# Three graph convolutions: node work done visit by visit inside the neighbour sums

## The chip, the cores and the metric

The kernel runs on one core of a Trainium2 chip. The metric is device microseconds (us) of one execution; shown are the median and the extremes of three executions. One further execution was profiled, and all rows below come from it.

## The reference, cut to what matters

The input is a graph of 12500 nodes with 32 features each and 200000 edges, sorted by destination. Four blocks follow one another, each of the form `x = x + block(relu(layernorm(x)))`: three graph convolutions in a row, an attention over edges, a relational convolution, and a tensor product. The change touches only the first block and the entry of the second:

```python
def _gcn_conv(x, src, dst, norm, W, b, n_nodes):
    h = x @ W
    msg = h[src] * norm[:, None]          # norm = dinv[src] * dinv[dst], self loops included
    out = jax.ops.segment_sum(msg, dst, num_segments=n_nodes)
    return out + b
h = jax.nn.relu(_gcn_conv(h, src, dst, norm, W1, b1, n))   # 32 -> 128
h = jax.nn.relu(_gcn_conv(h, src, dst, norm, W2, b2, n))   # 128 -> 128
h = jax.nn.relu(_gcn_conv(h, src, dst, norm, W3, b3, n))   # 128 -> 32
...
x = x + gcn;  h = relu(layernorm(x));  x = x + attention(h)   # its q, k, v are h @ Wq, h @ Wk, h @ Wv
```

All is float32. The kernel sums before or after the product with W, whichever is narrower, so its three neighbour sums are 32, 128 and 32 features wide.

## The kernel before, in words

Nodes lie in 98 tiles of 128 (J; arrays are padded to JP = 104). Edges lie in 98 groups (NG) of 2048: 128 partitions by 16 columns (GT). Since edges are sorted by destination, a group meets one to three node tiles; each meeting is a pair, called a visit here. There are 195 pairs and one empty visit, NS = 196. The table `group_words`, made once by `group_tables`, holds for each visit its group (W_NEED), its tile (W_TILE) and its ring slot (W_SLOT), and for each group the last visit that reads it (W_DONE).

A neighbour sum is `group_sums` (L907). Its engines run side by side, each in its own program order, held together by semaphores:

- GpSimd (POOL) issues 16 indirect DMAs for each group (L884), each of which gathers one row per partition from a DRAM table into a ring of two slots. A row is the float32 value split in three bfloat16 parts. POOL waits for `released`, which SyncE raises (L902) when ScalarE has copied the last visit of the group that held the slot. SyncE also stages the indices (L871) and counts landed groups (L897).
- ScalarE copies the slot into `rows`, one of two buffers, once for each visit (L945, and L944 for two columns of marks in the first sum).
- VectorE compares column numbers with the destinations and so makes a one-hot matrix in bfloat16 for each visit (L865), two visits ahead, in one of two buffers. After the products it joins the three parts (L959) and adds the result into the visit's tile of `sums` (L966).
- TensorE multiplies 16 one-hots with 16 columns of rows and accumulates them in PSUM (L979).

A sum ends with a barrier of all engines. Between sums the node work is done on all tiles at once: the own value of each node is added, `node_linear` (L1080) turns each tile with TensorE, multiplies it by the weights and copies it back, `on_vector` (L1191) applies scale, bias and relu in a chain of VectorE instructions, `store_parts` (L1048) splits the result in three parts and stores the table that the next sum gathers from. After the third sum come the residual, the layer norm of attention (`norm_relu`, L1006), the q, k, v product and the store of the key and value table `tab64`. `step_tables` (L490), which makes the per-edge tables that only later passes read, runs before `group_tables`.

The order is written out by hand; no planner is involved. The score pass of attention (L1302) begins with its own gathers on POOL.

Of the kernel before, what the change touches and what calls it, by code (L numbers as in the profile page):

```python
# [19 lines left out]
F32 = mybir.dt.float32  # L20
BF16 = mybir.dt.bfloat16
# [687 lines left out]
def group_tables(nc, k, dram):  # L709
# [3 lines left out]
    with ExitStack() as ctx:  # L713
# [28 lines left out]
        with nc.Block() as block:  # L742
# [17 lines left out]
            def _(dve):  # L760
# [24 lines left out]
                chain.link(nc.vector.memset(words[:, W_DONE, :], 1.0))  # L785
                chain.link(nc.vector.tensor_single_scalar(words[:, W_DONE, 0:NG], done[:], 1.0, op=ALU.add))
# [4 lines left out]
                nc.vector.tensor_single_scalar(shift[:], spread[:, 1, :], -float(P), op=ALU.mult).then_inc(set_up, 1)  # L791
                for c in range(NG // CH):
# [68 lines left out]


def _group_one_hot(nc, k, out, step):

    return nc.vector.tensor_tensor(out[:], k["columns"][:],  # L865
                                   k["group_rel"][:, bass.ds(step * GT, GT)].unsqueeze(1).to_broadcast([P, P, GT]), ALU.is_equal)


def _stage_half(sp, k, staged, indexed, turn, half):

    sp.dma_start(staged[:, half * HALF * GT:(half + 1) * HALF * GT],  # L871
                 k["group_src"][:, bass.ds((turn * SPAN + half * HALF) * GT, HALF * GT)]).then_inc(indexed[half], DMA)


def _gather_groups(nc, pool, table, staged, ring, slots, indexed, released, gathered, entered):

    with pool.Fori(0, ROUNDS) as i:
        for q in range(SPAN):
            if q % HALF == 0:
                pool.wait_ge(indexed[q // HALF], (i + 1) * DMA)  # L880
            pool.wait_ge(released, i * SPAN + q + 1)
            pool.sem_inc(entered, 1)
            for g in range(GT):
                nc.gpsimd.indirect_dma_start(  # L884
                    out=ring[:, q % slots, g, :], out_offset=None, in_=table,
                    in_offset=bass.IndirectOffsetOnAxis(ap=staged[:, q * GT + g:q * GT + g + 1], axis=0)).then_inc(gathered[q % HALF], DMA)


def _pass_groups(sp, k, staged, slots, indexed, gathered, landed, copied, released):

    sp.sem_inc(released, slots)
    for half in range(2):
        _stage_half(sp, k, staged, indexed, 0, half)
    with sp.Fori(0, ROUNDS) as i:
        for q in range(SPAN):
            sp.wait_ge(gathered[q % HALF], (i * 2 + q // HALF + 1) * GT * DMA)
            sp.sem_inc(landed, 1)  # L897
            if q % HALF == HALF - 1:
                _stage_half(sp, k, staged, indexed, i + 1, q // HALF)
            done = sp.value_load(k["group_words"][0:1, W_DONE, bass.ds(i * SPAN + q, 1)], min_val=1, max_val=NS)  # L900
            sp.wait_ge(copied, done)
            sp.sem_inc(released, 1)  # L902
    for half in range(2):
        sp.wait_ge(indexed[half], (ROUNDS + 1) * DMA)


def group_sums(nc, k, name, table, sums, width, marks=None, last=None):  # L907

    W = 3 * width
    held = W + (2 if marks is not None else 0)  # L910
    slots = 2
    with ExitStack() as ctx:
        sb, psum, sem = _scope(nc, ctx, name)
        staged = sb("staged", [P, SPAN * GT], U32)
        ring = sb("ring", [P, slots, GT, W], BF16)
        rows = [sb(f"rows{h}", [P, GT, held], BF16) for h in range(2)]
        onehot = [sb(f"onehot{h}", [P, P, GT], BF16) for h in range(2)]
        joined = [sb(f"joined{h}", [P, width]) for h in range(2)]
# [1290 lines left out]
```

## Time and profile before

| | us |
|---|---|
| Median of three executions | 16398.22 |
| Lowest and highest | 16385.13 and 16399.88 |
| Profiled execution, its time | 16390.01 |
| Its span | 16388.3 |
| POOL busy | 10536.2 (64%) |
| TensorE matmuls busy | 7263.1 (44%) |
| VectorE busy | 5726.5 (35%) |
| ScalarE busy | 2889.0 (18%) |
| Mean granted TensorE clock | 0.645 of full speed |

The engines' busy shares are means over stages that have different limits. To read them by stage, one asks for the busy time of each engine in stretches of the span, and for the order of instructions at the seams between stretches. In such a row the columns are the stretch, its length, then the busy time and instruction count of TensorE matmuls, TensorE weight loads, VectorE, ScalarE and POOL, the granted clock as a share of full speed, the busy share of the DMA engines and GB/s. In a timeline row the columns are start, duration, engine, line, operation, operands, count, and in brackets the idle time before it and what ended it.

### The profile page before, as it was taken

Reading aid. Unit: us, or ns where it says so; the run is one execution under the profiler, and the core shown is the slowest. Engines: PE = TensorE matmul, PEld = TensorE weight load, DVE = VectorE, ACT = ScalarE, POOL = GpSimd, SP = SyncE. Lnnn points to the kernel's source line nnn. Section 1 sums busy time; section 2 is a strip of 40 time slices with the busy share of each in tenths; the row PEclk is TensorE's granted clock in tenths of the full one; section 3 lists DMA queues with packets and bytes.
Section 4 is the critical chain, followed back from the end, with each engine's and each line's share of the span. In section 5 each row is a group of like instructions: output and inputs, shape, how many; then the busy total and the mean of one; then the engine's idle time right before and its main releaser. Section 6 shows DMA issues by size and latency. Waiting matters only on the chain. (4 is left out here: it accounts for less than half of the span.)

```text
span 16388.3 us, 210648 instructions
## 1 busy us (share of the span) xinstructions
PE 7263.1 (44%) x43306; PEld 5194.0 (32%) x43356; DVE 5726.5 (35%) x10642; ACT 2889.0 (18%) x3659; POOL 10536.2 (64%) x10566
## 2 busy tenths in 40 slices
PE   2311111233333111115555535558889867455556
PEld 1111111122222111114444423335555536333435
DVE  4511113111113111121111147767777742323332
ACT  1111111455551111110000000012222211000001
POOL 0377774677772777767777743346666652777774
PEclk8655555677675555555555555579999975777676
DMA  4111111322221111112222212211111112111112
GB/s 145 19 19 19 19 19 36 85 77 77 77 77 26 19 19 19 19 15 52 49 49 49 49 32 67 67 31 33 33 33 33 33 40 58 21 21 21 21 21 48
DMA packets 652644, 675.65 MB, mean 41 GB/s; under 512 B 303477, under 2 KB 489790, under 8 KB 649663
## 3 DMA queue, kind: packets, MB, share of 16 engines
q0 software_dynamic: 340624, 383.65, 12.6%
q1 hardware_dynamic: 280958, 278.52, 5.6%
q10 hardware_dynamic: 30384, 7.79, 0.3%
q14 instruction: 661, 5.41, 0.1%
q8 instruction: 17, 0.28, 0.0%
HBM read 517.39 MB, written 149.11 MB: 41 GB/s over the span
## 5 line engine op out<-in xcount | busy, mean ns | idle before, releaser
L884 POOL DMA_INDIRECT gcn_sum_ring<-scratch_parts,gcn_sum_staged x4704 | 4684.5, 996 | 1961.9 <-issue 1395.6
L979 PE MATMUL gcn_sum_totals<-gcn_sum_rows,gcn_sum_onehot 128*128 128x98 bf16 (+2 forms) x9408 | 1290.0, 319 | 5113.9 <-ACT gcn_sum_rows L945 5107.2
L979 PEld LDWEIGHTS gcn_sum_totals<-gcn_sum_rows,gcn_sum_onehot 128*128 128x128 bf16 x9408 | 973.0, 158 | 5431.5 <-issue 5365.5
L865 DVE TENSOR_TENSOR gcn_sum_onehot<-k_columns,k_group_rel 128x2048 bf16<-128x2048 bf16 x594 | 728.5, 1227 | 5041.1 <-PE gcn_sum_totals L979 4863.1
L703 POOL DMA_INDIRECT sh_ring<-scratch_tab,sh_staged x1664 | 1879.4, 1129 | 830.1 <-issue 506.9
L703 POOL DMA_INDIRECT rel_ring<-scratch_tab,rel_staged x1664 | 1702.4, 1023 | 832.5 <-issue 476.1
L945 ACT COPY gcn_sum_rows<-gcn_sum_ring 128x1536 bf16 (+1 forms) x588 | 1604.6, 2751 | 2924.3 <-SPq L897 2916.4
L1339 POOL DMA_INDIRECT score_ring<-scratch_tab,score_staged x1664 | 1737.5, 1044 | 533.2 <-issue 506.8
L642 PE MATMUL sh_accumulator<-sh_message,sh_onehot 128*128 128x248 f32 x3328 | 1209.7, 543 | 1245.6 <-DVE sh_message L2002 1242.4
L642 PE MATMUL rel_accumulator<-rel_message,rel_onehot 128*128 128x512 f32 x3328 | 1609.3, 628 | 2.8 <-ACT rel_accumulator L675 2.8
L642 PEld LDWEIGHTS sh_accumulator<-sh_message,sh_onehot 128*128 128x128 f32 x3328 | 950.6, 293 | 1504.1 <-issue 1326.4
L1748 DVE TENSOR_TENSOR rel_message<-rel_coef,rel_ring 128x512 f32<-128x512 f32 x1664 | 1044.9, 690 | 14.2
L1379 PE MATMUL score_q_edge<-att_h,score_onehot_t 128*128 x3328 | 752.4, 402 | 272.9 <-ACT score_onehot_t L1328 272.9
L642 PEld LDWEIGHTS rel_accumulator<-rel_message,rel_onehot 128*128 128x128 f32 x3328 | 635.1, 201 | 660.0 <-issue 654.6
L1379 PEld LDWEIGHTS score_q_edge<-att_h,score_onehot_t 128*128 128x128 f32 x3328 | 725.4, 330 | 355.2 <-issue 355.2
L1999 DVE TENSOR_TENSOR sh_message<-sh_parts,sh_ring 128x1024 f32<-128x1024 f32 x208 | 257.3, 1237 | 1659.5 <-DMA sh_ring<-scratch_tab,sh_staged 1659.5
L1373 PE MATMUL score_flipped_ps<-k_ident,score_onehot 128*128 128x128 f32 x1664 | 409.2, 427 | 822.5 <-DVE score_onehot L591 822.5
L1357 DVE TENSOR_TENSOR score_product<-score_q_edge,score_ring 128x256 f32<-128x256 f32 x208 | 88.4, 425 | 1779.4 <-DMA score_ring<-scratch_tab,score_staged 1779.4
L1598 POOL TENSOR_TENSOR value_message<-value_ring,att_score 128x256 f32<-128x256 f32 x208 | 183.3, 881 | 683.3 <-DVE value_parts L1622 478.8
L642 PE MATMUL value_accumulator<-value_parts,value_onehot 128*128 128x36 bf16 x4992 | 448.1, 199 | 371.3 <-issue 201.2
L1373 PEld LDWEIGHTS score_flipped_ps<-k_ident,score_onehot 128*128 128x128 f32 x1664 | 326.7, 224 | 850.3 <-DVE score_onehot L591 616.8
L1328 ACT COPY score_onehot_t<-score_flipped_ps 128x1024 f32<-128x1024 f32 x208 | 210.6, 1012 | 2043.6 <-PE score_flipped_ps L1373 2043.6
(393 smaller groups left out, 9375.7 us busy)
## 6 DMA issues: line engine op xcount, KB each, us to landing
gcn_sum_ring<-scratch_parts,gcn_sum_staged POOLq DMA_INDIRECT x4704
scratch_kv<-score_ring SPq DMA_DIRECT2D x208, 256.0 KB, 2.0
value_ring<-scratch_kv SPq DMA_DIRECT2D x208, 256.0 KB, 2.6
rel_ring<-scratch_tab,rel_staged POOLq DMA_INDIRECT x1672
score_ring<-scratch_tab,score_staged POOLq DMA_INDIRECT x1664, 2.5
sh_ring<-scratch_tab,sh_staged POOLq DMA_INDIRECT x1664, 2.4
scratch_totals<-rel_taken SPq DMA_DIRECT2D x102, 256.0 KB
rlo_lin_chunk<-scratch_totals SPq DMA_DIRECT2D x98, 256.0 KB, 2.9
```

The source lines that it names most:

```text
L642: last = self.nc.tensor.matmul(into, onehot, part, start=False, stop=True, skip_group_check=True)
L703: nc.gpsimd.indirect_dma_start(out=ring[:, q, g, :], out_offset=None, in_=table, in_offset=bass.IndirectOffsetOnAxis(ap=staged[:, q, g:g + ...
L865: return nc.vector.tensor_tensor(out[:], k["columns"][:], k["group_rel"][:, bass.ds(step * GT, GT)].unsqueeze(1).to_broadcast([P, P, GT]), ...
L884: nc.gpsimd.indirect_dma_start(out=ring[:, q % slots, g, :], out_offset=None, in_=table, in_offset=bass.IndirectOffsetOnAxis(ap=staged[:, ...
L945: nc.scalar.copy(rows[q % 2][:, :, 0:W], ring[:, bass.ds(slot, 1), :, :].rearrange("p o g w -> p (o g) w")).then_inc(copied, 1)
L979: done = nc.tensor.matmul(totals[:, q, 0:held], onehot[q % 2][:, :, g], rows[q % 2][:, g, :], start=(g == 0), stop=(g == GT - 1))
L1328: nc.scalar.copy(onehot_t[q % 2][:], flipped_ps[:, q % 2, :, :]).then_inc(turned[q], 1)
L1339: nc.gpsimd.indirect_dma_start(out=ring[:, q, g, :], out_offset=None, in_=dram["tab64"], in_offset=bass.IndirectOffsetOnAxis(ap=staged[:, ...
L1373: last = nc.tensor.transpose(flipped_ps[:, q % 2, g, :], onehot[q % 2][:, g, :], k["ident"][:])
L1379: last = nc.tensor.matmul(q_edge[:, q % 2, g * D:(g + 1) * D], onehot_t[q % 2][:, g, :], q_nodes[:, bass.ds(tiles[g] * D, D)], start=True, ...
L1748: nc.vector.tensor_tensor(message[m % 2][:, g, :].rearrange("p (b f) -> p b f", f=D), coef[m % 2][:, g, :].unsqueeze(2).to_broadcast([P, N ...
L1999: nc.vector.tensor_tensor(m[:, :, 0:4 * D].rearrange("p g (c f) -> p g c f", f=D), parts[:, q, :, 0:4].unsqueeze(3).to_broadcast([P, G, 4, ...
```

## The change

- The three sums become three functions, `first_sums`, `second_sums` and `third_sums`, that share a class `Gathered`. It holds what `group_sums` held: gathers, SyncE's control, the copies, the one-hots and the products are issued as before, with two PSUM buffers in place of four.
- The joined result is no longer added into an array of all tiles. A running sum of one tile is kept, `sums = sums * keep + joined`, where `keep` is 1 if this visit has the tile of the visit before, else 0.
- Behind it, each visit does the node work of its tile with the sum as it stands, a few visits late (`lag`): own value, dinv, a TensorE transpose, the weights, relu, the split in parts, and a store of 128 rows to the table, issued on ScalarE's queue. Where a tile has two visits, the later one overwrites what the earlier one stored. The third sum does residual, layer norm, q, k, v and the store of keys and values in this way.
- Removed: the node work between the sums, the clearing of the arrays of sums, the store and reload of the wide own values (`tab128`), and the node work at the entry of attention.
- Weights are loaded once, ahead of the first sum. The bias b1 is a 33rd row of W1, b2 is a product of a row of ones with b2.
- `step_tables` is moved behind the third sum. `group_tables` makes `keep`. W_DONE counts from an offset (BASE = 16).

The core of the diff:

```diff
-        group_sums(nc, k, "gcn_sum0", dram["parts32"], sums, D, marks=k["marks"], last=last)
...
-        node_linear(nc, k, "gcn_lin1", sums[:].rearrange("p j f -> p (j f)"), JP // 4, 1, w1, wide[:].rearrange("p j f -> p (j f)"))
-        on_vector(nc, "gcn_act1", [
...
-        store_parts(nc, "gcn_parts1", dram["parts128"], wide, HID)
-        store_table(nc, "gcn_table1", dram["tab128"], wide, HID)
...
+    def fold(self, dve, k, m, q):
+
+        dve.wait_ge(self.multiplied, m + 1 + BASE)
+        self.nc.vector.tensor_reduce(self.joined[q % 2][:], self.totals[:, q % 2, 0:3 * self.width].rearrange("p (c f) -> p f c", c=3),
+                                     axis=AX_X, op=ALU.add).then_inc(self.folding, 1)
+        dve.wait_ge(self.folding, m + 1)
+        self.nc.vector.scalar_tensor_tensor(out=self.sums[q % 2][:], in0=self.sums[(q + 1) % 2][:], scalar=k["keep"][:, bass.ds(m, 1)],
+                                            in1=self.joined[q % 2][:], op0=ALU.mult, op1=ALU.add).then_inc(self.folded, 1)
...
+            _linked(dve, scaling, m + 1, nc.vector.tensor_tensor(held[q % 2][:], got.sums[q % 2][:], _tile(h, tile), ALU.add))
+            dve.wait_ge(flipped, m - 1 + BASE)
+            nc.vector.tensor_scalar(scaled[q % 2][:], held[q % 2][:], k["dinv"][:, bass.ds(tile, 1)], None, ALU.mult).then_inc(summed, 1)
+
+        def split_rows(dve, m, q):
...
+            nc.vector.tensor_copy(_tile(wide, tile), raised[q % 2][:])
+            _linked(dve, splitting, 2 * m + 1, nc.vector.tensor_tensor(rest[q % 2][:], raised[q % 2][:], high, ALU.subtract))
+            _linked(dve, splitting, 2 * m + 2, nc.vector.tensor_copy(middle, rest[q % 2][:]))
+            nc.vector.tensor_tensor(low, rest[q % 2][:], middle, ALU.subtract).then_inc(split, 1)
...
+            nc.scalar.activation(parts[q][:, 0:HID], linear_ps[:, 0:HID], ACT.Relu, scale=k["dinv"][:, bass.ds(tile, 1)]).then_inc(activated, 1)
...
+            act.dma_start(dram["parts128"][bass.ds(tile * P, P), :], parts[q][:]).then_inc(stored, DMA)
...
@@ second_sums, ScalarE @@
+                def body(n, q):
+                    if _live(n, 0):
+                        got.copy_rows(act, k, n, q)
+                    if _live(n, 2):
+                        turn(act, n - 2, (q + 2) % 4)
+                    if _live(n, 3):
+                        activate(act, n - 3, (q + 1) % 4)
+                    if _live(n, 4):
+                        turn_again(act, n - 4, q)
+                    if _live(n, 7):
+                        store(act, n - 7, (q + 1) % 4)
...
@@ third_sums, VectorE @@
+                def body(n, q):
+                    if _live(n, 0):
+                        got.make_one_hot(dve, k, n, q)
+                    if _live(n, 2):
+                        normalize(dve, n - 2, (q + 2) % 4)
+                    if _live(n, 1):
+                        add_own(dve, n - 1, (q + 3) % 4)
+                    if _live(n, 4):
+                        take_query(dve, n - 4, q)
```

In the third sum `add_own` is the fold and nine more VectorE instructions, each waiting for the one before (own value, scale with bias, relu with residual, mean, centring, square, variance), and `normalize` three (reciprocal, scale with relu, add to x).

## Rows read from the trace of the kernel before

**Rows 1.** Stretches: us, PE, PEld, DVE, ACT, POOL busy, clock, DMA, GB/s.
```profile
192.50:282.50 90.00, 36.11 (x156) 31.12 (x156) 17.76 (x83) 28.71 (x39) 12.33 (x13) 0.65 0.79 258
561.00:634.90 73.90, 0.00 (x0) 0.00 (x0) 47.13 (x43) 0.29 (x1) 0.03 (x1) 0.50 0.34 56
634.90:2709.10 2074.20, 290.04 (x3088) 257.27 (x3088) 343.89 (x965) 303.76 (x386) 1596.43 (x1568) 0.51 0.14 19
2709.10:2910.40 201.30, 35.56 (x126) 17.23 (x126) 126.86 (x80) 10.44 (x32) 7.51 (x27) 0.59 0.27 82
2910.40:4914.90 2004.50, 699.08 (x3088) 448.52 (x3088) 384.00 (x579) 1016.15 (x193) 1527.04 (x1568) 0.70 0.29 77
4914.90:5244.50 329.60, 149.42 (x636) 106.22 (x636) 129.85 (x247) 61.09 (x199) 55.94 (x196) 0.61 0.11 28
5244.50:7283.20 2038.70, 280.42 (x3088) 252.18 (x3088) 306.05 (x579) 280.51 (x193) 1560.94 (x1568) 0.51 0.14 19
7283.20:7406.20 123.00, 30.52 (x126) 17.64 (x126) 63.90 (x56) 10.42 (x30) 7.44 (x26) 0.62 0.12 28
```

**Rows 2.** Costliest groups, gathers and a one-hot: busy us, mean ns, idle.
```profile
L884 POOL DMA_INDIRECT gcn_sum_ring<-scratch_parts,gcn_sum_staged x4704 | 4684.5, 996 | 1961.9 <-issue 1395.6
L1339 POOL DMA_INDIRECT score_ring<-scratch_tab,score_staged x1664 | 1737.5, 1044 | 533.2 <-issue 506.8
...
L591 DVE TENSOR_TENSOR score_onehot<-k_iota,k_drel 128x1024 f32<-128x1024 f32 x209 | 254.4, 1218 | 5.2
```

**Rows 3.** Second sum, POOL's waits: us, times, longest; line 884: ns least/median/greatest.
```profile
POOL gcn_sum_ring L884 <- issue: 453.9, 1490, 0.3
POOL gcn_sum_ring L884 <- SPq L902: 23.4, 77, 0.3
...
L884 POOL DMA_INDIRECT gcn_sum_ring<-scratch_parts,gcn_sum_staged x4704: 940/944/1991, 634.9 to 7282.1; - x196
```

**Rows 4.** Timeline, first sum: two gathers beside one-hots.
```profile
659.69 1.23 DVE L865 TENSOR_TENSOR gcn_sum_onehot<-k_columns,k_group_rel 128x2048 bf16<-128x2048 bf16 x1 [25.30 <-PE gcn_sum_totals L979]
659.86 1.87 POOL L884 DMA_INDIRECT gcn_sum_ring<-scratch_parts,gcn_sum_staged  x1 [0.30 <-issue]
...
662.73 1.23 DVE L865 TENSOR_TENSOR gcn_sum_onehot<-k_columns,k_group_rel 128x2048 bf16<-128x2048 bf16 x1 [1.12 <-issue]
663.28 1.49 POOL L884 DMA_INDIRECT gcn_sum_ring<-scratch_parts,gcn_sum_staged  x1 [0.30 <-issue]
```

**Rows 5.** Timeline, second sum: ScalarE's copies of one group.
```profile
3400.16 0.94 POOL L884 DMA_INDIRECT gcn_sum_ring<-scratch_parts,gcn_sum_staged  x1 [0.30 <-issue]
3401.82 10.53 ACT L945 COPY gcn_sum_rows<-gcn_sum_ring 128x6144 bf16 x2 [9.61 <-SPq L897]
```

**Rows 6.** Timeline, end of the first sum.
```profile
2707.97 0.94 POOL L884 DMA_INDIRECT gcn_sum_ring<-scratch_parts,gcn_sum_staged  x1 [0.30 <-issue]
2710.89 1.47 ACT L945 COPY gcn_sum_rows<-gcn_sum_ring 128x1536 bf16 x1
2716.81 1.22 DVE L865 TENSOR_TENSOR gcn_sum_onehot<-k_columns,k_group_rel 128x2048 bf16<-128x2048 bf16 x1 [0.73 <-issue]
2722.38 0.48 DVE L1164 MEMSET gcn_w<- 128x512 f32 x1 [0.99 <-PEq L99]
```

**Rows 7.** Timeline, end of the second sum: ScalarE.
```profile
4916.90 15.75 ACT L945 COPY gcn_sum_rows<-gcn_sum_ring 128x6144 bf16 x3 [15.23 <-SPq L897]
```

**Rows 8.** Timeline, start of the second sum.
```profile
2906.57 1.16 SPq L871 DMA_DIRECT2D gcn_sum_staged<-k_group_src  x2
2910.31 0.97 POOL L884 DMA_INDIRECT gcn_sum_ring<-scratch_parts,gcn_sum_staged  x1 [142.84 <-DMA gcn_sum_staged<-k_group_src]
```

**Rows 9.** Groups by shape, 561 to 7404 us: small operations.
```profile
L966 DVE TENSOR_TENSOR gcn_sums<-gcn_sums,gcn_sum_joined 128x32 f32 x392 | 75.3, 192 | 28.0
L966 DVE TENSOR_TENSOR gcn_sums<-gcn_sums,gcn_sum_joined 128x128 f32 x196 | 57.3, 292 | 28.0
L1126 PE MATMUL gcn_lin_flipped_ps<-k_ident,gcn_lin_chunk 128*128 128x128 f32 x222 | 62.1, 374 | 132.1 <-POOL gcn_lin_chunk L1116 129.4
L1143 ACT COPY gcn_lin_turned<-gcn_lin_flipped_ps 128x128 f32<-128x128 f32 x222 | 51.1, 267 | 281.8 <-PE gcn_lin_flipped_ps L1126 281.8
```

More of the change, by code:

```diff
@@ L860, in _ @@
                 nc.scalar.activation(k["dinv"][:], k["dinv"][:], ACT.Sqrt)
[L863 to L872, printed above, removed]
@@ L875, in _gather_groups @@
[L875 to L886, printed above, removed]
@@ L889, in _pass_groups @@
[L889 to L904, printed above, removed]
@@ L1238, in gcn, with _live, _pairs, _word_of @@
-def gcn(nc, io, k, dram):
+BASE, AHEAD = 16, 8
+def _live(n, lag):
+    return not isinstance(n, int) or 0 <= n - lag < NS
+def _pairs(engine, body, lag):
+    for n in range(AHEAD):
+        body(n, n % 4)
+    with engine.Fori(0, (NS - AHEAD) // 4) as i:
+        for q in range(4):
+            body(i * 4 + q + AHEAD, q)
+    for n in range(NS, NS + lag):
+        body(n, n % 4)
+def _word_of(engine, k, row, n, low, high):
+    return engine.value_load(k["group_words"][0:1, row, bass.ds(n, 1)], min_val=low, max_val=high)
@@ new lines, in _tile_of, with _tile, _pair_one_hot, _gather_groups @@
+def _tile_of(engine, k, n):
+    return _word_of(engine, k, W_TILE, n, 0, J)
+def _tile(a, tile):
+    return a[:, bass.ds(tile, 1), :].rearrange("p o f -> p (o f)")
+def _pair_one_hot(nc, k, out, n):
+    return nc.vector.tensor_tensor(out[:], k["columns"][:],
+                                   k["group_rel"][:, bass.ds(n * GT, GT)].unsqueeze(1).to_broadcast([P, P, GT]), ALU.is_equal)
+def _gather_groups(nc, pool, table, staged, ring, slots, indexed, released, gathered, entered):
+    with pool.Fori(0, ROUNDS) as i:
+        for q in range(SPAN):
+            if q % HALF == 0:
+                pool.wait_ge(indexed[q // HALF], (i + 1) * DMA)
+            pool.wait_ge(released, i * SPAN + q + 1)
+            pool.sem_inc(entered, 1)
+            for g in range(GT):
+                nc.gpsimd.indirect_dma_start(
+                    out=ring[:, q % slots, g, :], out_offset=None, in_=table,
+                    in_offset=bass.IndirectOffsetOnAxis(ap=staged[:, q * GT + g:q * GT + g + 1], axis=0)).then_inc(gathered[q % HALF], DMA)
@@ new lines, in _stage_half, with _pass_groups @@
+def _stage_half(sp, k, staged, indexed, turn, half):
+    sp.dma_start(staged[:, half * HALF * GT:(half + 1) * HALF * GT],
+                 k["group_src"][:, bass.ds((turn * SPAN + half * HALF) * GT, HALF * GT)]).then_inc(indexed[half], DMA)
+def _pass_groups(sp, k, staged, slots, indexed, gathered, landed, copied, released):
+    sp.sem_inc(released, slots)
+    for half in range(2):
+        _stage_half(sp, k, staged, indexed, 0, half)
+    with sp.Fori(0, ROUNDS) as i:
+        for q in range(SPAN):
+            sp.wait_ge(gathered[q % HALF], (i * 2 + q // HALF + 1) * GT * DMA)
+            sp.sem_inc(landed, 1)
+            if q % HALF == HALF - 1:
+                _stage_half(sp, k, staged, indexed, i + 1, q // HALF)
+            done = sp.value_load(k["group_words"][0:1, W_DONE, bass.ds(i * SPAN + q, 1)], min_val=BASE + 1, max_val=NS + BASE)
+            sp.wait_ge(copied, done)
+            sp.sem_inc(released, 1)
+    for half in range(2):
+        sp.wait_ge(indexed[half], (ROUNDS + 1) * DMA)
@@ L1283, in gcn @@
[L1283 to L1293 removed]
+        w1 = sb("w1", [D + 1, HID])
```

599 lines of the change are left out of this document (428 added, 171 removed).

## The prediction, made before the result was known

> **What bounds the kernel now.** I first asked for the busy times by stretch, because the busy shares of the whole span mix stages. The three neighbour sums take 2074, 2004 and 2039 us, and in each POOL is busy 1527 to 1596 us while no other engine passes 1016 [rows 1]. POOL's idle time there is about 477 us in each sum, 0.30 us ahead of each of 1568 gathers, and no single idle time is longer [rows 1, 3]: it never waits for a slot. So a sum is bound by issuing gathers, one each 0.944 + 0.305 = 1.249 us [rows 3, 4], 1958 us in all, plus what lengthens single gathers. A gather has a median of 944 ns and a greatest of 1991 [rows 3]; the lengthening is 1596 - 1568 x 0.944 = 116 us in the first sum, 47 in the second, 81 in the third [rows 1], together 244.
>
> Then I read the seams. Between the last gather of one sum and the first of the next there are 201.3, 329.6 and (to attention's first gather) 123.0 us, in which POOL does 7.5, 56 and 7.4 us of copies [rows 1]. Node work lies open there. These 654 us are what the change can take; the sums' 6117 us are what it can spoil.
>
> **Removed and added at the seams.** What stays of a seam is the drain of the last visits and the setup of the next sum.
>
> - First seam. The last gather ends at 2708.9, the copies start 1.8 us later, and the old sum was over at 2721.4 (the next instruction, at 2722.38, had idled 0.99) [rows 6]. Now three visits and their late steps drain. ScalarE needs for a visit a copy of 1.47, a turn of 0.27, two activations of some 0.3 and a store's issue of 0.4 to 0.6 (SyncE's two took 1.16 [rows 8]), with register loads 3.9 us; VectorE needs a one-hot of 1.23, five small operations of the fold and four of the split at 0.16 to 0.29 [rows 4, 9], with loads about 4.5 us. The last copy ends 9.5 us after the first starts, its products 1.5 later, its fold at 13, then flip 0.4, turn 0.3, product 0.4, activations 0.7, split 1.7, store about 2.5: 19.5 us. The three small steps on `last`, with barriers of about 1 us, take 3, and from staging to first gather 3.7 us pass [rows 8]. Sum 1.8 + 19.5 + 3 + 3.7 = 28. Gain 173.
> - Second seam. Three copies took 15.75 us [rows 7]; with 2.3 us of new ScalarE work between them they take 20.5. Products of 3.6, fold 2, flip, turn, two products, activation, second flip and turn, narrow product (each 0.27 to 0.4 [rows 9], with signals 4.5), split and store 3.7: 34. With landing, barrier and staging 39.5. Gain 290.
> - Third seam. Bound by VectorE: one-hot 1.23, some fourteen small operations at about 0.22 with the wait between them, and three register loads of up to 0.7 (0.73 is the idle ahead of a one-hot [rows 6]) make about 7 us for a visit. The drain is 24 us, with landing and barriers 28. Gain 95. Residual, norm, q, k, v and table store lie within this seam's 123 us and go.
> - `step_tables` moves past the sums. It takes 90.0 us with nothing beside it [rows 1] and will take the same between the third sum and attention: its 13 gathers on POOL, its transposes and its SyncE stores have no neighbour in either place. 0; if SyncE's stores were late, at most a few us.
> - Front. Nine weight loads at 0.4 us issue each plus about 3 us to land, less a cleared array of 2.8 us: +5.
>
> Seams and front: 173 + 290 + 95 - 5 = 553 us gained.
>
> **Added beside the gathers.** All per-visit work lies beside POOL's 1.249 us beat. A group takes about 20.4 us and mostly has two visits, so an engine has 10.2 us for one.
>
> - ScalarE, second sum: 5.3 for the copy [rows 5] and about 2.3 of new work, 7.6 us. Its order decides when the ring slot is released. The next group's first gather began at 3400.16, the group's two copies ended at 3412.35 [rows 5], and POOL needs their slot 16 gathers, 20.0 us, after 3400.16: 7.8 us are spare and 2.3 are used. In a group of three visits the copies alone take 15.75 and 4.6 come between: late by about 2 us, in the few such groups. +4. The stores queue on ScalarE, each waits for the one before, and a copy queued behind would wait; a visit lies between them, so I take 0, at worst 2 us a visit, within the 7.8.
> - VectorE: 4.5, 5 and 7 us a visit. TensorE adds two to four float32 operations of 0.37 us [rows 9] to 16 products of about 0.22. Both under 10.2. What is queued behind the new waits are the next visits' products and one-hots; POOL does not wait for those while copies go through.
> - Lengthened gathers. This is the price that counts. At 659.86 a gather that starts 0.17 us after a one-hot takes 1.87 us, and at 663.28 one takes 1.49; both end 0.81 us after the one-hot's end (660.92 and 663.96) [rows 4]. So a gather needs something at about 0.13 us after its start that the one-hot holds until it ends. If phases are spread evenly, an operation of d us covers that instant with chance d/1.25 and costs d/2, thus d²/2.5: 0.605 us for a one-hot, 119 a sum. Measured: 116, 47, 81, or 244/588 = 0.415 us for each. In the score loop, whose one-hots are as long, the lengthening is (1044 - 944) ns x 1664 = 166 us, 0.80 for each of 208 [rows 2]. The order of VectorE's work is new, so I do not keep 0.415 but go toward the even value and take 588 x 0.5 = 294; bounds 0.24 (the second sum now, 141) and 0.80 (the score loop, 470). The small operations with SBUF operands, about seven a visit at 0.19 to 0.29 [rows 9], cost by the same formula 0.014 to 0.034 each, 82 us; I take 60, since some fall where a gather has just been held up. Bounds 0 and, if each held the gather for its whole length, 4.35 us over the three sums' visits x 196 = 853. Term: 294 + 60 - 244 = +110.
>
> The row on the one-hot is weighed against the Trainium skill, page "SBUF — State Buffer", section "Who interferes with whom": a tensor_tensor with two SBUF inputs blocks only GpSimd instructions that read SBUF, and descriptor generation is inferred not to suffer; copies, casts and tensor_scalar in a two-port mode do block it, for their whole length. The trace disagrees on the one-hot, a tensor_tensor: it lengthens gathers. By the page the new subtractions and additions would be free and the term 30 us lower, and only the new copies, casts and scalings would count.
>
> **Sum.** 16390.0 - 553 + 4 + 110 = 15951, with the 8 us by which the median stands above the profiled execution 15959. I forecast 15960. By the bounds of the lengthening that are likely: 15,850 (one-hots at 0.24, small ones at half) to 16,110 (0.80).
>
> **Rivals.**
> - A. Small operations hold the gathers fully, so that every new VectorE instruction is paid on POOL: + 853 - 60 on the forecast, 16,750, slower. It decides from (553 - 4 + 244 - 294)/588 = 0.85 us more a visit. For it: the one-hot does block until its end [rows 4], and the page on SBUF quoted above says so of two-port operations. Against: a gather begun first ran on unhindered, and the median stays at 944 [rows 3]. 5%.
> - B. An in-order engine can't do a visit in 10.2 us, and POOL waits for slots: likeliest ScalarE in the second sum, waiting behind stores, or VectorE in the third. At 11.5 us a visit in one sum the price is 1.3 x 196 = 255: 16,215. Against: the 7.6 and 7 above. 6%.
> - C. The drains are deep: each of five to seven late steps waits for the slowest engine, 60 us more a seam: 16,140. For it: 8 to 14 waits along one visit. 8%.
> - D. The new order falls into a phase that spares the gathers, as the second sum now: 588 x 0.24 + 20 - 244 = -83 in place of +110: 15,770. 8%.
>
> The forecast has 73%. The 80% range 15,850 to 16,110 reaches halfway to C and D. Less than 0.2% (33 us) can't be told from no change here. Faster by more: all but A and some of B, 93%; same 2%; slower 5%.
>
> **What would show it.** Steps: first gathers of the second and third sum 28 and 40 us after the last of the sum before; step_tables 90 us, now after the third sum; POOL's idle in each sum still near 477 us, and none by SyncE's release; POOL's busy sum in the three loops near 4440 + 354 = 4800 us. I am wrong if POOL's idle grows (B), if its busy sum passes 5100 (A), or if a seam is over 80 us (C).

## The result, and the profile after

The changed kernel takes 15,866.2 us (median of four, 15,846.7 to 15,883.2); the kernel before took 16,399.1 beside it. The ratio is 0.9675, 95% interval 0.9664 to 0.9687. The profiled execution, 15,883.2 us, is the slowest of the four; its span is 15,881.5, 506.8 less than before. In five of the runs below (e1 to e4 and h1) the kernel before, too, took some 19,300 us, so that their times can't be set beside the others.

The stretches, as in [rows 1]; the last row is `step_tables`, now inside the third seam:

```profile
471.00:548.80 77.80, 0.00 (x0) 0.00 (x0) 45.16 (x47) 0.29 (x1) 0.07 (x1) 0.50 0.33 55
548.80:2574.50 2025.70, 473.65 (x3662) 364.62 (x3662) 593.32 (x1918) 433.63 (x957) 1548.03 (x1568) 0.50 0.16 29
2574.50:2604.30 29.80, 9.28 (x62) 6.79 (x62) 12.98 (x46) 9.15 (x23) 0.13 (x1) 0.50 0.11 33
2604.30:4671.00 2066.70, 1234.07 (x4612) 721.17 (x4612) 696.26 (x1905) 1145.98 (x763) 1577.34 (x1568) 0.70 0.29 77
4671.00:4724.10 53.10, 25.88 (x92) 16.06 (x92) 14.92 (x56) 20.49 (x21) 0.10 (x1) 0.60 0.04 10
4724.10:6770.50 2046.40, 466.53 (x3659) 358.99 (x3659) 818.33 (x3066) 372.51 (x763) 1568.74 (x1568) 0.50 0.14 22
6770.50:6899.70 129.20, 45.91 (x221) 37.81 (x221) 34.62 (x154) 36.33 (x60) 12.31 (x14) 0.51 0.57 182
6808.20:6898.20 90.00, 35.72 (x156) 30.52 (x156) 17.70 (x82) 28.64 (x39) 12.19 (x13) 0.52 0.80 258
```

The seams went from 201.3, 329.6 and 123.0 us to 29.8, 53.1 and 39.2 (129.2 less the 90.0 of `step_tables`), the front from 73.9 to 77.8: 531.8 - 3.9 = 527.9 us gained. The three sums grew from 6117.4 to 6138.8 us, +21. Net 506.5, the difference of the spans.

What the +21 is, the profile's rows for the gathers tell (busy us, mean ns of one, idle us before them):

```profile
L1136 POOL DMA_INDIRECT sum0g_ring<-scratch_parts,sum0g_staged x1568 | 1548.1, 987 | 833.9 <-issue 832.1
L1136 POOL DMA_INDIRECT sum1g_ring<-scratch_parts,sum1g_staged x1568 | 1577.5, 1006 | 519.1 <-issue 472.2
L1136 POOL DMA_INDIRECT sum2g_ring<-scratch_parts,sum2g_staged x1568 | 1568.8, 1001 | 530.7 <-issue 461.4
```

Busy less 1568 x 0.944 is the lengthening: 68, 97 and 89 us, together 254, where before had 116, 47 and 81, together 244 [rows 1, 3]. The other part is a wait that before did not have. The second sum's waits (us, times, longest):

```profile
PE sum_narrow_ps L1470 <- DVE sum_parts L1419: 520.9, 188, 3.1
ACT sum_turned_again L1438 <- PE sum_narrow_ps L1470: 233.1, 91, 3.1
POOL sum1g_ring L1136 <- SPq L1160: 17.1, 18, 5.1
```

The last row is POOL waiting for a ring slot: 17.1 less 18 usual pauses of 0.305 leaves 11.6 us. The other two rows name its cause, and the end of that sum shows it in single instructions:

```profile
4678.82 5.33 ACT L1197 COPY sum1g_rows<-sum1g_ring 128x6144 bf16 x1
...
4686.72 0.19 DVE L1419 TENSOR_TENSOR sum_parts<-sum_rest,sum_parts 128x32 bf16<-128x32 f32 x1
...
4687.05 0.60 PE L1470 MATMUL sum_narrow_ps<-gcn_w,sum_turned_again 128*128 128x32 f32 x2 [2.86 <-DVE sum_parts L1419]
...
4687.69 0.27 ACT L1438 COPY sum_turned_again<-sum_flipped_again_ps 128x128 f32<-128x128 f32 x1 [3.06 <-PE sum_narrow_ps L1470]
...
4690.30 5.31 ACT L1197 COPY sum1g_rows<-sum1g_ring 128x6144 bf16 x1 [2.34 <-DMA scratch_parts<-sum_parts]
```

TensorE's narrow product of visit n-4 waits until VectorE has split visit n-5, and VectorE does that only a turn later, behind its fold. ScalarE's second turn waits for the narrow product, and its next copy stands in line behind: 11.5 us from one copy's start to the next, where the copy takes 5.3.

### The profile page after: what moved, and what is told of

It is laid out like the page before. It is cut to its first block and busy times, and to the rows that moved or that the text cites. A ratio compares the mean times of both kernels' runs of the same rounds, so it can differ in the third digit from the quotient of the medians.

```text
span 15881.5 us, 235812 instructions
## 1 busy us (share of the span) xinstructions
PE 8010.6 (50%) x45355; PEld 5572.4 (35%) x45356; DVE 6520.0 (41%) x15205; ACT 3194.9 (20%) x5174; POOL 10462.7 (66%) x10318
## 5 line engine op out<-in xcount | busy, mean ns | idle before, releaser
L703 POOL DMA_INDIRECT sh_ring<-scratch_tab,sh_staged x1664 | 1875.2, 1127 | 830.2 <-issue 506.8
L1136 POOL DMA_INDIRECT sum0g_ring<-scratch_parts,sum0g_staged x1568 | 1548.1, 987 | 833.9 <-issue 832.1
L1136 POOL DMA_INDIRECT sum1g_ring<-scratch_parts,sum1g_staged x1568 | 1577.5, 1006 | 519.1 <-issue 472.2
L1136 POOL DMA_INDIRECT sum2g_ring<-scratch_parts,sum2g_staged x1568 | 1568.8, 1001 | 530.7 <-issue 461.4
L1197 ACT COPY sum1g_rows<-sum1g_ring 128x6144 bf16 x196 | 1042.1, 5318 | 680.0 <-SPq L1155 599.7
L1211 PE MATMUL sum0g_totals<-sum0g_rows,sum0g_onehot 128*128 128x98 bf16 x3136 | 299.5, 285 | 1638.7 <-ACT sum0g_rows L1197 1638.7
L1211 PE MATMUL sum1g_totals<-sum1g_rows,sum1g_onehot 128*128 128x384 bf16 x3136 | 944.5, 487 | 331.6 <-ACT sum1g_rows L1197 325.8
L1809 PE MATMUL score_q_edge<-k_q,score_onehot_t 128*128 x3328 | 752.6, 402 | 272.7 <-ACT score_onehot_t L1758 272.7
L1809 PEld LDWEIGHTS score_q_edge<-k_q,score_onehot_t 128*128 128x128 f32 x3328 | 725.5, 331 | 355.2 <-issue 355.2
L1211 PE MATMUL sum2g_totals<-sum2g_rows,sum2g_onehot 128*128 128x96 bf16 x3136 | 294.4, 283 | 886.2 <-ACT sum2g_rows L1197 818.2
L1211 PEld LDWEIGHTS sum1g_totals<-sum1g_rows,sum1g_onehot 128*128 128x128 bf16 x3136 | 492.2, 163 | 709.6 <-issue 413.3
```

The costliest lines, as they stand in the source:

```text
L703: nc.gpsimd.indirect_dma_start(out=ring[:, q, g, :], out_offset=None, in_=table, in_offset=bass.IndirectOffsetOnAxis(ap=staged[:, q, g:g + ...
L1136: nc.gpsimd.indirect_dma_start(out=ring[:, q % slots, g, :], out_offset=None, in_=table, in_offset=bass.IndirectOffsetOnAxis(ap=staged[:, ...
L1197: self.nc.scalar.copy(self.rows[q % 2][:, :, 0:3 * self.width], self.ring[:, bass.ds(slot, 1), :, :].rearrange("p o g w -> p (o g) w")).th ...
L1211: last = self.nc.tensor.matmul(self.totals[:, q % 2, 0:self.held], self.onehot[q % 2][:, :, g], self.rows[q % 2][:, g, :], start=(g == 0), ...
L1809: last = nc.tensor.matmul(q_edge[:, q % 2, g * D:(g + 1) * D], onehot_t[q % 2][:, g, :], q_nodes[:, bass.ds(tiles[g] * D, D)], start=True, ...
```

## The experiments

In the profiles of e1 to e4 and of h1 register instructions on VectorE, ScalarE, TensorE and SyncE lasted several times as long in bursts (in h1 the mean of VectorE's assert instruction was 0.122 us against 0.023), and POOL waited for slots. These profiles are read for how single gathers stand to single VectorE operations. Their sums of lengthening can be compared with each other only: e3 had 145 us and f3, the same kernel, 269, perhaps because POOL's waits change where the gathers fall; no run shows that.

**The gathers' lengthening: no one-hot, quarters, and a third lever (e1 to e4).**

```diff
# e1: later visits of sums 2 and 3 reuse what the buffer holds
-        _pair_one_hot(...).then_inc(self.made, 1)
+        dve.sem_inc(self.made, 1)
# e2: quarters
+        for c in range(0, P, 32):
+            last = nc.vector.tensor_tensor(onehot[:, c:c + 32, :], k["columns"][:, c:c + 32, :], ..., ALU.is_equal)
# e3: second sum, VectorE
-                    if _live(n, 6):
-                        split_rows(dve, n - 6, (q + 2) % 4)
+                    if _live(n, 5):
+                        split_rows(dve, n - 5, (q + 3) % 4)
# e4: quarters, and in sums 1 and 3 the column numbers lie in PSUM
+        self.columns = psum("columns", [P, 4, P // 4, GT]) if width == D else None
```

> The changed kernel without the one-hots of the second and third sum, save the first two of each: stale one-hots are multiplied, so those sums are wrong numbers. Theory T1: the lengthening of gathers beside the new per-visit work comes from the 1.23 us one-hots alone; the lengthening beyond 0.944 us a gather falls from 97 and 89 us in those two sums to under 15 us each, and is about 68 us as before in the first, which keeps its one-hots; total 15866 - 160 = 15705. Theory T2: the new small operations (0.16 to 0.35 us each, 9 to 15 a visit) carry a share by the d*d/2.5 formula of the prediction; then 25 to 30 us stay in each of the two sums, total about 15740. Theory T3: small operations hold gathers for their whole length: over 200 us would stay in each; already unlikely.

> The changed kernel with each one-hot made in four instructions of 32 nodes (about 0.35 us each) instead of one of 1.23 us, in all three sums. T1, each instruction holds back only a gather whose early instant falls into it, until that instruction ends: a hit costs at most 0.35 us instead of 1.23, so the lengthening falls from 254 us to 588 x 4 x 0.35*0.35/2.5 = 115 us or less: total about 15730 to 15780. Rival: instructions back to back hold the gather as one (it gets in only when VectorE pauses): lengthening unchanged or larger, 15870 to 15930.

> Second sum only: split_rows runs five visits late instead of six. In the changed kernel TensorE's narrow product of visit n-4 waits for the split of n-5, which VectorE does only in its turn n+1, behind the fold of visit n; ScalarE's second turn and the next copy wait for that. Theory S: this chain (copy, products, fold, split, narrow, turn, copy) sets 9.7 us a visit in the drain and in groups of three visits; with lag five the second seam falls from 53 us to about 42 and the 11.6 us of POOL waits for slots in the second sum vanish: total 15 to 25 us less, 15845. Rival: the drain is set by the copies of 5.3 us and the products of 5.3 us at the low clock, and changes by under 4 us.

> As e2 (four instructions for a one-hot), and in the first and third sum the column numbers that it compares are read as float32 from PSUM instead of bfloat16 from SBUF, so that only one operand comes from SBUF; the second sum is as in e2. T1a: a gather is held back by an instruction with two SBUF operands; with one, the lengthening in the first and third sum falls to what the small operations give, under 15 us each. T1b: any long VectorE instruction holds it back: then it is as in e2 or larger, since these instructions may be slower (0.5 to 0.6 us). VectorE has room for both. Total by T1a about 15700, by T1b 15780 to 15850.

Measured times 19,695, 19,696, 19,792 and 19,686 us, ratios to before 1.017, 1.017, 1.023 and 1.018. None of the expected times can be judged by them, and why these kernels are slower than the one before there was not found. The lengthening by sum was 30, 7 and 3 us in e1; 17, 27 and 22 in e2; 28, 59 and 57 in e3; 2, 19 and -1 in e4. The first sum of e1 and e3 is that of the changed kernel, where it has 68 us, so even untouched it has less than half here. Beside e3 the others still show the order: without one-hots next to nothing is left, quarters cut it, and with one operand in PSUM it is gone. All four were measured again (f1 to f3, g1; e4's lever is within f1).

**The changed kernel once more (c0).**

> The changed kernel unaltered, as the control for the four variants run before, whose chip ran the kernel before in 19329 us instead of 16399, with register instructions of 0.7 us in bursts where they take 0.05 to 0.15 otherwise. If this control falls on a chip with such bursts: by theory R the change issues more register work for each visit on ScalarE and VectorE (a load of the tile's number for each step), so that the bursts put it over the time a group leaves, and the changed kernel takes 19700 to 19850 against 19329 of before, the variants' changes being small beside that. The rival: the variants themselves made it slower, and the control is near 18800. If it falls on a chip without bursts: 15866 as first measured.

15,867.6 us (15,858.5 to 15,872.7), ratio 0.9672 [0.9656, 0.9688]; lengthening 67, 92 and 81, seams 30 and 50. The result stands, on another occasion. The long register instructions did not occur, so what was expected of them stays untested. The second seam is 3 us shorter than in the profile of after, with no edit: TensorE was granted 0.67 of its clock in it and 0.60 there, and the 16 products of a visit took 4.1 to 4.4 us against 4.7 to 5.3. So the second seam of another run is to be compared with the one of the two that had a like clock.

**The same levers again (f1, f2, f3).** f2 is e2's kernel and f3 is e3's; f1 has quarters, columns in PSUM and the earlier split together.

> Two edits of the changed kernel together: split_rows of the second sum five visits late instead of six, and one-hots in four instructions, with the column numbers read as float32 from PSUM in the first and third sum (in an earlier run on a slowed chip the lengthening there fell to 1.5 and -0.8 us, in the second sum, in quarters but from SBUF, to 19). Base is the changed kernel at 15867, lengthening 240 to 254 us. T1a (a VectorE instruction with two SBUF operands holds back a gather, one with a single SBUF operand doesn't): lengthening 5 + 45 + 5 us, minus 190; with the shorter chain another 15 to 25: 15655. T1b (any long instruction does): about 15760. If VectorE, now slower in its one-hots, became the bound in the third sum, POOL would show waits for SyncE's release there and the gain would be under 100.

> One-hots in four instructions of 32 nodes, both operands in SBUF; the rest is the changed kernel. The d*d/2.5 formula gives 588 x 4 x 0.35*0.35/2.5 = 115 us of lengthening for 240 to 254 now: 15735. The rival, back-to-back instructions that hold the gather as one: 15870 or more.

> split_rows of the second sum five visits late instead of six, nothing else. Theory S (the narrow product waits for a split that stands behind the next visit's fold on VectorE): second seam 53 to about 42 us, POOL's waits over 0.35 us in the second sum (3 of them, 10 to 12 us) gone, 15 to 25 us in all: 15847. Rival (copies and products set the drain): under 4 us.

f2 took 15,693.2 us (15,677 to 15,713), ratio 0.9566 [0.9551, 0.9582]. Its gathers:

```profile
L1136 POOL DMA_INDIRECT sum0g_ring<-scratch_parts,sum0g_staged x1568 | 1492.5, 952 | 832.9 <-issue 831.7
L1136 POOL DMA_INDIRECT sum2g_ring<-scratch_parts,sum2g_staged x1568 | 1506.8, 961 | 528.3 <-issue 463.8
L1136 POOL DMA_INDIRECT sum1g_ring<-scratch_parts,sum1g_staged x1568 | 1511.3, 964 | 519.1 <-issue 468.8
```

Lengthening 12, 31 and 27: 70 in place of 254, and less than the 115 expected, so the price d²/2.5 is too high. f1 took 15,669.6 us (15,660 to 15,672), 0.9551 [0.9535, 0.9567]:

```profile
L1136 POOL DMA_INDIRECT sum0g_ring<-scratch_parts,sum0g_staged x1568 | 1484.4, 947 | 833.0 <-issue 830.8
L1136 POOL DMA_INDIRECT sum1g_ring<-scratch_parts,sum1g_staged x1568 | 1512.2, 964 | 512.3 <-issue 474.3
L1136 POOL DMA_INDIRECT sum2g_ring<-scratch_parts,sum2g_staged x1568 | 1480.1, 944 | 522.0 <-issue 462.9
```

4 and 0 us in the sums whose columns lie in PSUM, though a quarter lasts 0.68 us there against 0.42; 32 in the second. That the columns are float32 there is not what does it: the score pass compares float32 with float32, both in SBUF, and its gathers are lengthened (160 us, and 27 in quarters, see g2).

f3 took 15,876.7 us (15,869 to 15,882), 0.9677 [0.9661, 0.9693]: no gain, though its edit did what it should. The narrow product's wait is gone from the second sum's waits, POOL's wait for slots there (us, times, longest) is

```profile
POOL sum1g_ring L1136 <- SPq L1160: 4.6, 10, 1.8
```

1.5 us in place of 11.6. The seam is 46.8 us, at a granted clock of 0.61. Beside after, at 0.60, that is 6.3 us less; c0, the changed kernel at 0.67, had 50.0:

```profile
4679.60:4726.40 46.80, 22.43 (x92) 14.79 (x92) 13.97 (x51) 20.19 (x21) 0.09 (x1) 0.61 0.05 11
4663.70:4713.70 50.00, 22.22 (x92) 14.61 (x92) 14.91 (x56) 20.26 (x21) 0.03 (x2) 0.67 0.05 11
```

The first row is f3, the second c0. But VectorE's work now stands elsewhere against the gathers, and the lengthening in that sum went from 97 to 122 us. What one gave the other took: the expected 15,847 was missed by 30 us.

**One part of the change alone (f4).** The first sum as changed, the second and third as before (the functions of the kernel before, which come with it, are left out of the cut):

```diff
-            second_sums(nc, k, dram, wide, w2, b2, w3, own)
-        third_sums(nc, k, dram, own, b3, w, x_next, q_nodes)
+            store_table(nc, "gcn_table1", dram["tab128"], wide, HID)
+    old_rest(nc, io, k, dram, x_next, q_nodes)
```

> One part of the change alone: the first sum as in the changed kernel (node work in its visits), then the wide table is stored and the second and third sum, the node work between them and attention's entry are as in the kernel before; step_tables stays behind them. If the seams' gains add up: the first seam keeps its drain (30 us), the store of the wide table (27) and the clearing (12), so 201 becomes about 70, minus 131; the first loop's lengthening goes from 116 to 68, minus 48; loads and a copy of x plus 6: 16405 - 173 = 16232. If moving step_tables or the new order of weight loads were worth something by itself, the sum would miss by that much.

16,229.8 us (16,227 to 16,231), 0.9893 [0.9876, 0.9909]. That is 2 us from what was expected. The first seam is 69 us there, since the wide table is still stored in it and the array cleared; the lengthening is 67, 54 and 82 us. So the gains of the seams add up, and moving `step_tables` is worth nothing that could be seen.

**The one-hots left out, again (g1), and the levers put on later loops (g2).** g1 is e1's kernel (its edit keeps the one-hots of two visits in each sum, not of four). g2 is f1 and this:

```diff
+    for g in range(0, G, 2):
+        last = nc.vector.tensor_tensor(out[:, g:g + 2, :], k["iota"][:]..., k["drel"][:, bass.ds(first + g, 2)]..., ALU.is_equal)
...
+                        for g in range(0, G, 2):
+                            at = slice(g, g + 2)
+                            nc.vector.tensor_tensor(m[:, at, 0:4 * D]..., ALU.mult)
```

> The changed kernel, but VectorE makes the one-hots of the second and third neighbour sums only for the first four visits (each buffer filled); later visits use what the buffer holds, so the sums' numbers are not the reference's. All the small operations of VectorE stay. Theory (only the one-hots lengthen gathers): the lengthening falls from 97 us to under 10 in the second sum and from 89 to under 10 in the third, the first stays at 68; the time is 15866 - 176 = about 15,690. Rival (the small operations of the fold, the split and the layer norm carry half or more of it): 45 us or more stay in each, 15,770 or above. Second rival (VectorE freed of 1.23 us a visit changes the drains): the two later seams fall from 53 and 39 us by more than 3 us each.

> The changed kernel with one-hots of the neighbour sums in quarters (column numbers in PSUM in the first and third sum), split of the second sum one visit later, and besides this the one-hots of the attention's score pass, and of the tensor product pass at the end with its message multiplications, each issued in four pieces. The first three measures alone gave 15,670 us. Theory (a gather is lengthened to the end of whatever VectorE operation covers its first 0.13 us, so pieces cost about a quarter in the most, since POOL's other gathers fall between them): the lengthening of the score pass falls from 160 us to about 50, that of the tensor product pass from some 310 to about 100, and the time to about 15,360. Rival (pieces issued back to back hold a gather as one): the lengthening stays, and the time is 15,670 or, with the pieces' own starts on VectorE, 15,700.

g1 took 15,713.8 us (15,701 to 15,726), 0.9583 [0.9567, 0.9599], 24 above the 15,690 expected (19 of them are more lengthening in the tensor product's loop, which the edit does not touch):

```profile
L1136 POOL DMA_INDIRECT sum1g_ring<-scratch_parts,sum1g_staged x1568 | 1486.2, 948 | 521.2 <-issue 472.2
L1136 POOL DMA_INDIRECT sum2g_ring<-scratch_parts,sum2g_staged x1568 | 1480.0, 944 | 527.3 <-issue 461.7
```

6 and 0 us, with every small operation of VectorE still in place: the first rival, that these carry half, falls. The second seam is 49.8 us at a granted clock of 0.67, where c0 had 50.0 at 0.67: the drain does not hang on the one-hot.

g2 took 15,351.6 us (15,333 to 15,355), 0.9360 [0.9344, 0.9375], the fastest kernel of the study, 515 us below the changed one.

```profile
L711 POOL DMA_INDIRECT sh_ring<-scratch_tab,sh_staged x1664 | 1713.0, 1029 | 830.0 <-issue 506.8
L1788 POOL DMA_INDIRECT score_ring<-scratch_tab,score_staged x1664 | 1598.3, 961 | 525.8 <-issue 506.5
```

Against 1664 x 0.944 the score pass is lengthened by 27 us (160 in f1) and the tensor product pass by 142 (327 in f1), where about 50 and 100 had been expected. That is 318 us less, and the times of f1 and g2 differ by 318.

**A rule read from the traces, and its test (h1).** Why do quarters cost less than d²/2.5 says (4 x 588 x 0.42²/2.5 = 165 us, measured 70), and small operations nearly nothing? I sorted all gathers by where they start against a one-hot. In the kernel before, 114 of 4704 gathers start from 0.13 us before to 0.03 us after a one-hot's start; none is lengthened. 453 start later than 0.05 us into one and reach their 0.13 us mark before it ends; 450 of them are lengthened, and each ends 0.81 to 0.83 us after the one-hot's end. Two cases of the changed kernel's second sum, 0.04 and 0.03 us after the start:

```profile
3026.65 1.23 DVE L1123 TENSOR_TENSOR sum1g_onehot<-k_columns,k_group_rel 128x2048 bf16<-128x2048 bf16 x1
3026.69 2.00 POOL L1136 DMA_INDIRECT sum1g_ring<-scratch_parts,sum1g_staged  x1 [0.30 <-issue]
...
3323.61 1.29 DVE L1123 TENSOR_TENSOR sum1g_onehot<-k_columns,k_group_rel 128x2048 bf16<-128x2048 bf16 x1
3323.64 0.95 POOL L1136 DMA_INDIRECT sum1g_ring<-scratch_parts,sum1g_staged  x1 [0.30 <-issue]
```

In the first the gather waits, in the second the one-hot does, for some 0.07 us. So both seem to reach for one thing (what it is, no trace shows), the gather about 0.13 us after its start and the one-hot about 0.17 after its own; who is first has it, the gather briefly, the one-hot to its end. In f2's third sum the same holds for the four quarters of a one-hot (one row, x4): the gather 0.04 us after the start goes through, the next, begun in the last quarter, is held by 0.09 us to that quarter's end:

```profile
5275.47 1.50 DVE L1204 TENSOR_TENSOR sum2g_onehot<-k_columns,k_group_rel 128x512 bf16<-128x512 bf16 x4 [0.47 <-issue]
5275.51 0.94 POOL L1136 DMA_INDIRECT sum2g_ring<-scratch_parts,sum2g_staged  x1 [0.30 <-issue]
...
5276.76 1.03 POOL L1136 DMA_INDIRECT sum2g_ring<-scratch_parts,sum2g_staged  x1 [0.30 <-issue]
```

And in f1's first sum, with the columns in PSUM, 311 gathers start later than 0.05 us into a quarter, reach their mark before it ends, and none is held:

```profile
597.28 2.48 DVE L1209 TENSOR_TENSOR sum0g_onehot<-sum0g_columns,k_group_rel 128x512 bf16<-128x512 f32 x4
597.29 0.94 POOL L1136 DMA_INDIRECT sum0g_ring<-scratch_parts,sum0g_staged  x1 [0.30 <-issue]
598.54 0.94 POOL L1136 DMA_INDIRECT sum0g_ring<-scratch_parts,sum0g_staged  x1 [0.30 <-issue]
```

A comparison of d us thus costs (d - 0.17)²/2.5 at even phases, not d²/2.5. For 588 one-hots that is 588 x 1.055²/2.5 = 262 us (244 before, 254 after), in quarters 4 x 588 x 0.249²/2.5 = 58 (70), for an operation of 0.29 us 0.006, for one of 0.19 nothing.

```diff
-        for c in range(0, P, 32):
+        for c in range(0, P, 16):
```

> The changed kernel with each one-hot of the three sums issued in eight pieces of 16 columns in place of one. From 1.225 us for the whole and 0.419 for a quarter a piece should take 0.15 + 0.134 = about 0.285 us, 2.3 for a one-hot. In the traces so far a gather that starts while a one-hot runs is held to its end, but only if it starts more than about 0.04 us after the one-hot's start: one whose 0.13 us mark falls in the first 0.17 us of a one-hot is never held. Theory (that grace holds for each piece by itself): with even phases a piece of d us costs (d - 0.17)^2 / 2.5, so 588 one-hots cost 262 us whole (254 measured), 59 in quarters (70 measured) and 8 x 588 x 0.0053 = 25 in eighths; a held gather is lengthened by at most 0.12 us; the time is 15,693 - 45 = about 15,650. Rival 1 (no grace, cost d^2 / 2.5 a piece): 152 us of lengthening and 15,775. Rival 2 (once in pieces, what is left is a fixed price of each one-hot): 70 us and 15,693. Rival 3 (VectorE gets too late with 1.1 us more a visit): POOL's waits for slots in the second sum grow from 12 us.

19,610 us, before 19,263: its time can't be used. Its gathers:

```profile
L1136 POOL DMA_INDIRECT sum0g_ring<-scratch_parts,sum0g_staged x1568 | 1493.5, 952 | 1384.5 <-issue 821.3
L1136 POOL DMA_INDIRECT sum1g_ring<-scratch_parts,sum1g_staged x1568 | 1497.8, 955 | 1308.6 <-SPq L1160 797.7
L1136 POOL DMA_INDIRECT sum2g_ring<-scratch_parts,sum2g_staged x1568 | 1492.7, 952 | 1108.6 <-SPq L1160 582.7
```

13, 18 and 13: 44 us, where e2, quarters in a profile of this kind, had 66 and e3, whole, 145. The sum decides little, since sums of such profiles are not those of the others; the form without the free 0.17 us was already out by f2 (165 against 70). The single gathers decide more. With quarters in f2, 2 of 91 gathers whose mark falls 0.10 to 0.16 us into a later piece of a one-hot are lengthened, and none of 48 in a first piece: the free time holds for each piece. (All 39 whose mark falls into the first 0.06 us of a later piece are held, for the piece before still runs then: quarters start 0.335 us apart and last 0.42.) In eighths none of 37 are in a first piece, but 102 of 247 in a later one, by 0.20 us on the mean and 20.7 us in all, about as much as 44 is above the 25 of the rule. So for pieces of 0.285 us the theory fails in part, and why was not found. Eighths start 0.20 us apart. The third rival, VectorE too late, can't be judged here, since POOL waited for slots in the other four profiles of this kind as well; the eight pieces took 1.70 us of VectorE's time, not the 2.3 expected.

## Why the prediction was right, and which terms were not

The forecast for the profiled execution was 15,951; it was 15,883.2. By the prediction's own terms: seams and front 25 us less gained, slots 8 more, lengthening 100 less; 15,951 + 25 + 8 - 100 = 15,884. The median, 15,866, lies 94 below the 15,960 and inside both bounds, 16 above the lower one. Part of that closeness is errors of opposite sign. And the lower bound does not follow from what is said to give it: one-hots at 0.24 and small ones at half are 153 and 30 us less than the forecast, 15,777 and not 15,850.

- **What bounds the kernel: right.** POOL's idle time is 477.5 us in the first and third sum, as before, and 489.3 in the second. Nothing else of the new work reached POOL.
- **First seam: right,** 29.8 us against 28.
- **Second seam: 53.1 against 39.5,** the gain 276 in place of 290. The step that failed is the drain worked out along one visit, copies and then late steps in a row. It left out that the narrow product must wait for the split of the visit before. f3, which splits one visit earlier, takes 6.3 us of the 13.6 back at a like clock (0.61 and 0.60); f1, at 0.69, has 44.5 us, 5.5 less than c0 at 0.67. The clock itself is worth 3 us, as c0 shows. Read from the trace of after, the third copy ends 22.6 us after the first begins, against 20.5 reckoned, and the last store is issued 22.7 us after that, against 13.5; the last four stores stand 1.68 us apart, each waiting for the one before. No run tested that part.
- **Third seam: 39.2 against 28.** `step_tables` took 90.0 us in its new place, as forecast (in c0, f2 and f3 it was 5 us shorter: the seam with it is 124 us in place of 129.2, with its first gather at the same 38.3). The drain lasts 33 us from the first copy (6772.3) to the last stores (6803.5 to 6805.5), where 24 were reckoned. A turn is about as long as forecast, 6.3 us (the q, k, v products of the last visits start at 6779.6, 6786.0, 6792.3 and 6798.3), but there are more turns of it: the late steps of a visit wait, one after another, for TensorE and VectorE to come round. That is read from the trace; no run tested it.
- **Front: right,** +3.9 against +5.
- **Slots in the second sum: 11.6 us against 4.** I gave three-visit groups 2 us each. The trace has only four of them, the last with no group behind it, and three waits, one behind each of the others. The longest is 5.1, since the narrow product's wait lengthens ScalarE's turn. f3 shows the cause: with that wait gone 1.5 us are left.
- **Lengthened gathers: +10 against +110, the term that was mis-sized.** The step said that a one-hot holds a gather over all its length, chance d/1.25 and cost d/2, and took 0.5 us each, and 60 us for the small operations. The first 0.17 us of a one-hot hold nothing: 0.446 us for each one-hot at even phases. Of the 254 us measured, 247 lie on gathers whose mark a one-hot covers, 0.42 for each, and 7 on all others. So of the 100 us 47 are the one-hots (forecast 294) and 53 the small operations (forecast 60), which cost next to nothing (g1: 0 and 6 us with all of them in place). This also settles rival A, which had 16,750.
- **The row on the one-hot: measurement and notes differ.** The one-hot has two operands in SBUF and holds gathers; with one operand in PSUM it does not, as f1 shows in 311 cases. The Trainium skill, page "SBUF — State Buffer", section "Who interferes with whom", says the same of one SBUF input, and of two that they hold only instructions that read SBUF; its inference that descriptor generation does not suffer fails here. It also says that casts and tensor_scalar can hold the port in a two-port mode, and the trace does not speak against it. In the changed kernel's second sum a tensor_scalar of 0.29 us (L1407, 128 x 128 float32) held all 10 gathers whose mark came 0.234 us or more after its start, by 8 to 58 ns, and none of 42 before; in the first sum a cast of 0.23 us (L1281) held 16 of the 17 whose mark came 0.177 us or later, by up to 49 ns, and none of 85 before. In the third sum 34 gathers had their mark 0.16 to 0.22 us into a tensor_scalar of 0.24 us; none was lengthened, and the tensor_scalar took up to 0.30. One of the ten, which ends 0.82 us after the tensor_scalar's end:

```profile
4196.69 0.28 DVE L1407 TENSOR_SCALAR sum_scaled<-sum_held,k_dinv 128x128 f32<-128x128 f32 x1 [0.23 <-DVE sum_held L1405]
4196.80 1.00 POOL L1136 DMA_INDIRECT sum1g_ring<-scratch_parts,sum1g_staged  x1 [0.30 <-issue]
```

- **Rivals B, C and D: not so.** No engine missed its 10.2 us for long (B), the drains cost 27 us more in all and not 60 a seam (C). D had 0.24 us for each one-hot in all three sums; only the first went that way, from 116 us to 68, while the second went from 47 to 97. The time lies halfway between D's 15,770 and the forecast, but not by D's mechanism: more than half of the 100 us are the small operations.

Two things stay open. What set off the long register instructions was not found. And the lengthening of a loop depends on its phase against VectorE: the tensor product's loop, which no sum's edit touches, had 304 us in the profile of after and 323 to 327 in g1 and f1. Such shifts may be behind the 37 us between the four executions of after; no run shows that.

## What to carry to other kernels

Where GpSimd issues indirect DMAs back to back, look at the spread of one DMA's duration before its mean: here a greatest value near 1.23 + 0.81 us was a VectorE operation of 1.23 us with two SBUF operands standing in the way, and pieces of such an operation, or one operand in PSUM, take most or all of the cost away although VectorE gets busier. Price a drain by following the waits of each engine's turn, not the work of one visit. An edit that saves a wait can be paid back by a shift of phase, so compare the lengthening as well as the wait. And look at the granted clock of a stretch before its change is put down to an edit: one kernel had a seam of 53.1 us and one of 50.0.

## What the runs showed of the hardware that was not expected

- A 128 x 2048 bfloat16 comparison of 1.23 us on VectorE lengthens a GpSimd indirect DMA from 0.944 to as much as 2.00 us, but only one that starts more than 0.03 to 0.05 us after it; begun earlier, the DMA runs in 0.94 and the comparison takes up to 1.30.
- With its columns in PSUM, as float32, a quarter takes 0.68 us in place of 0.42 and holds no DMA.
- Pieces of one operation overlap in the profile: quarters last 0.42 us each but start 0.335 apart, and the four take 1.43 us in place of 1.23; eighths last 0.285, start 0.20 apart and take 1.70. So each further piece adds about 0.07 us.
- A tensor_scalar of 0.29 us and a cast of 0.23 us held gathers too, by at most 58 ns, and only when the gather's 0.13 us mark came in their last 0.05 us.
- In five runs register instructions of four engines lasted several times as long in bursts, and kernels of 16,400 us took 19,300.
